# Two attention layers on one core: head scores as fp32 row-tile products instead of stacked fp16 products

## The chip, the cores and the metric

The kernel runs on one core of a Trainium2 chip. The metric is the device time of one execution in microseconds (us); times here are medians of several runs. Engines are named PE (TensorE), ACT (ScalarE), DVE (VectorE), POOL (GpSimd) and SP (the engine that issues most transfers).

## The reference, cut to what matters

The input is x, fp32 of shape (2, 256, 64, 64): two images, 256 channels, N = 4096 positions. Layer 0 is multi-head attention over the positions, layer 1 a non-local block with a pooled key side; the change concerns layer 0 only.

```python
# layer 0: 8 heads of d = 32 channels, n = 4096 positions
qkv = einsum('oc,bchw->bohw', w_qkv, x); q, k, v = split(qkv, 3)
scores = einsum('bhdi,bhdj->bhij', q, k) / sqrt(d)
out = einsum('bhij,bhdj->bhdi', softmax(scores, axis=-1), v)
x = einsum('oc,bchw->bohw', w_proj, out) + x
# layer 1: softmax(theta(x[:, :64])^T maxpool(phi(x[:, 64:]))) times maxpool(g(x)), 1x1 convolution, batch norm, + x
```

## The kernel before, in words

A loop over the two images runs `layer0` and then `layer1`. `layer0` handles the eight heads in two groups of four (g = 0, 1), so there are four rounds of projections and attention in all.

Projections of a group (lines 257 to 388). PE makes q and k in 16 products of 128 channels by 512 positions (line 276) and then v (line 290). ACT writes each q or k piece as fp16 `hi` (line 306) and its square (line 311), and DVE writes the fp16 rest `lo` (line 328). A bound on the largest score is formed from the squares (lines 265, 323, 338 to 346) and stored in `safe`. SP then issues 24 transfers (line 384), which stack hi, lo, hi of every head in rows 0 to 95 of `Qst` and hi, hi, lo in `Kst`: one product over 128 rows then gives hi·hi + lo·hi + hi·lo. POOL clears the rows above (lines 360 to 365). The block ends when the transfers have landed.

Then every engine loads `safe` (line 393). Where the bound is too large, a block finds each query's maximum and puts it in row 96; in the profiled execution it isn't entered, since the page has no row of its lines. It works on the same stacked tensors, so that the attention is the same afterwards.

Attention of a group (lines 469 to 615). Queries go in 8 chunks of 512 (`CH`), keys in 32 tiles of 128 (`JT`). I call one key tile of one chunk a step. A step has four score products, one for each head (line 477, keys as weights, a PSUM bank of 128 keys by 512 queries each), exponentials from PSUM into `P` (line 563), four value products (line 487), and the row sums. The score banks form three buffers of two banks (`buf`, `NBUF` = 3), and one exponential empties one buffer. The value product of head h takes V's 32 columns of that head as weights and writes partitions 32h to 32h+31 of `psO`: four column tiles of the array. `P` is a ring of four key tiles.

Row sums: for most key tiles DVE adds `P` to one of two accumulators (line 595, `acc`), and for the key tiles in `SUM_PE` = 9, 20 and 31 PE sums `P` with a matrix of ones (line 500). At the end of a chunk PE also sums the two accumulators; I call these two groups the flushes. Output and sums are copied out by ACT (lines 534 and 539) inside the next chunk.

Each engine runs its own list in order, and semaphores join them: `s_ready` (scores ready), `s_exp` (exponentials done), `s_pv` (values done), `s_add` (DVE's adds), `s_sum` (PE's sums). PE's list is made from the exponentials' numbers: after exponential o it issues the scores of exponential o + 3, two products at a time (line 474 waits for the exponential that frees that buffer), and the value group of a key tile one exponential after its last one. The first exponential of a step also waits until values, adds and sums have freed the ring slot it writes (lines 552 to 560).

Of the kernel before, what the change touches and what calls it, by code (L numbers as in the profile page):

```python
# [5 lines left out]
ALU = mybir.AluOpType  # L6
# [8 lines left out]
N = H * W  # L15
CT = C // 128
HEADS, D = 8, 32
G = 4
# [11 lines left out]
MW = 1024.0  # L30
# [6 lines left out]
SCORE = 1.0 / (QS * QS * float(D) ** 0.5)  # L37

RING = 4
SIZES = ([2, 2] * 15 + [2, 1, 1]) * 2  # L40
NBUF = 3
NOPS = len(SIZES)
UNITS = JT * G
STARTS = [sum(SIZES[:o]) for o in range(NOPS)]
SUM_PE = [9, 20, 31]
# [18 lines left out]

DONE_BY = [next(o for o in range(NOPS) if STARTS[o] + SIZES[o] >= G * (j + 1)) for j in range(JT)]


VALUES_AT = [d + 1 for d in DONE_BY]
SUMS_AT = [DONE_BY[j] + 2 for j in SUM_PE]
ACC_AT = [NOPS + 1, NOPS + 3]  # L70
O_AT, L_AT = 3, 8
WORK = [(at, "values", j) for j, at in enumerate(VALUES_AT)]
WORK += [(at, "sums", j) for j, at in zip(SUM_PE, SUMS_AT)]
WORK += [(at, "acc", k) for k, at in enumerate(ACC_AT)]
TAIL = max(at for at, _, _ in WORK) + 1 - NOPS
ORDER = sorted((w for w in WORK if w[1] != "values"), key=lambda w: w[0])
FIRST_SUM, LAST_SUM = ORDER[0][1:], ORDER[-1][1:]
assert all(at >= DONE_BY[j] for at, what, j in WORK if what != "acc") and FIRST_SUM[0] == "sums"
assert NOPS % NBUF == 0 and sum(SIZES) == UNITS and SUM_V[:4] == [0, 1, 2, 3]


def conv_seq(nc, x, wqkv, wproj, gw, tw, pw, ww, vectors, biases, out, r_dram, r1_dram):
# [3 lines left out]
    with ExitStack() as root:  # L86
# [35 lines left out]
        safe = sb(root, "safe", [1, 1], I32)  # L122
# [107 lines left out]
        def layer0(b):  # L230
            with ExitStack() as ctx:
                Qst = sb(ctx, "Qst", [128, G, N], F16)
                Kst = sb(ctx, "Kst", [128, G, N], F16)
                V = sb(ctx, "V", [128, JT, G * D])
                s_x = [sem(ctx, f"s_x{c}") for c in range(NC)]
                s_pad = sem(ctx, "s_pad")
                s_mm = sem(ctx, "s_mm")
                s_ev = sem(ctx, "s_ev")
                s_hi = sem(ctx, "s_hi")
                for g in range(NG):  # L240

                    with ExitStack() as c2:
                        hi = [sb(c2, f"hi{k}", [128, N], F16) for k in range(2)]
                        lo = [sb(c2, f"lo{k}", [128, N], F16) for k in range(2)]
# [10 lines left out]
                        s_z = sem(c2, "s_z")  # L255
                        NU = 2 * NC
                        with nc.Block() as block:
# [62 lines left out]
                            def _(dve):  # L320
# [73 lines left out]
                    with ExitStack() as c2, nc.If(known_safe < 1):  # L394
# [9 lines left out]
                        with nc.Block() as block:  # L404
                            @block.gpsimd
                            def _(pool):
                                pool.sem_inc(s_m, 2)
# [669 lines left out]
```

## Time and profile before

| | |
|---|---|
| median of 3 runs | 2954.68 us (2951.5 to 2955.72) |
| span of the profiled execution | 2952.2 us |
| PE, DVE, ACT busy | 2823.0, 2357.6, 2351.8 us |
| instructions | 46817 |

The profiled execution has no time of its own in the list of runs: its span, from the first to the last instruction, is 2952.2 us and lies inside the range of the three runs. The median of the runs is 2.5 us above that span.

The page cuts the span in 40 slices. Engine rows give the busy share in tenths, and PEclk the clock that TensorE was granted:

```profile
PE   7999999999999999788979999999899999997889
DVE  3888888868888888677548888888588888886765
ACT  4999999958999999428449999999599999994284
PEclk9999999999999999899989999999999999999999
DMA  6000000030000000101150000000400000001011
```

Four stretches of attention fill most of the slices, in pairs; the DMA row shows the load of x and the stacking transfers ahead of each. What ends last in the attention is read from the rows further down. A matmul on fp32 data stands as two records in the trace (8192 records of line 487 for 4096 products).

### The profile page before, as it was taken

The page shows a single profiled execution, that of the slowest core. Times are in us where ns is not written, and L with a number is a line of the kernel's source. Part 1 is how long each engine was busy: PE and PEld are TensorE (multiplying, and loading weights), DVE is VectorE, ACT ScalarE, POOL GpSimd, SP SyncE. Part 2 cuts the span into 40 slices and gives each one's busy share as a digit, 9 for nine tenths or more (in the row PEclk, how much of TensorE's full clock was granted, in tenths as well). Part 3 has the DMA queues.
Part 4 walks back from the last instruction along what each step waited for, and adds up shares of the span by engine and source line. Part 5 has one row for each costly group of instructions (what it writes and reads, how often), then busy time and mean ns, then how long its engine had stood idle before and what let it go on. Part 6 is the DMA issues. An engine that isn't in the chain of part 4 may idle for free. (4 is left out here: it accounts for less than half of the span.)

```text
span 2952.2 us, 46817 instructions
## 1 busy us (share of the span) xinstructions
PE 2823.0 (96%) x16210; PEld 812.3 (28%) x16218; DVE 2357.6 (80%) x1478; ACT 2351.8 (80%) x2618; POOL 115.1 (4%) x148
## 2 busy tenths in 40 slices
PE   7999999999999999788979999999899999997889
PEld 4222222242222222233442222222422222222334
DVE  3888888868888888677548888888588888886765
ACT  4999999958999999428449999999599999994284
POOL 3000000010000000001030000000100000000010
PEclk9999999999999999899989999999999999999999
DMA  6000000030000000101150000000400000001011
GB/s 162 1 0 0 0 0 0 1 82 6 1 0 0 0 0 0 46 25 44 39 147 1 0 0 0 0 0 1 86 1 1 0 0 0 0 1 57 14 44 43
DMA packets 29171, 59.40 MB, mean 20 GB/s; under 512 B 11872, under 2 KB 12960, under 8 KB 25632
## 3 DMA queue, kind: packets, MB, share of 16 engines
q1 hardware_dynamic: 29088, 58.33, 7.3%
q8 instruction: 48, 0.79, 0.1%
q14 instruction: 35, 0.29, 0.0%
HBM read 22.88 MB, written 8.68 MB: 11 GB/s over the span
## 5 line engine op out<-in xcount | busy, mean ns | idle before, releaser
L563 ACT ACTIVATE P<-scores 128x1024 f32<-128x1024 f32 (+1 forms) x2112 | 1990.7, 1001 | 172.0 <-PE scores L477 155.6
L595 DVE TENSOR_TENSOR acc<-acc,P 128x2048 f32<-128x2048 f32 x800 | 1776.9, 2283 | 53.4 <-ACT P L563 50.6
L477 PE MATMUL scores<-Qst,Kst 128*128 (+1 forms) x4096 | 1090.8, 385 | 21.9 <-PEq L128 16.1
L487 PE MATMUL psOL<-P,V 128*32 128x512 f32 x8192 | 1090.4, 605 | 0.0
L477 PEld LDWEIGHTS scores<-Qst,Kst 128*128 128x128 f16 x4096 | 313.3, 98 | 1194.2 <-ACT P L563 752.4
L595 DVE TENSOR_TENSOR acc<-P 128x2048 f32<-128x2048 f32 x64 | 146.8, 2293 | 226.1 <-ACT P L563 119.3
L487 PEld LDWEIGHTS psOL<-P,V 128*32 128x32 f32 x8192 | 162.1, 108 | 432.2 <-ACT P L563 327.7
L276 PE MATMUL scores<-X,wq_sb 128*128 128x512 f32 x256 | 124.0, 614 | 29.2 <-DMA X<-in_x 25.4
L997 DVE SCALAR_TENSOR_TENSOR Pl<-O,Ph 128x1536 f16<-128x1536 f32 (+1 forms) x48 | 75.9, 1581 | 65.7 <-ACT Ph L970 65.7
L963 ACT ACTIVATE O<-scores 128x1536 f32<-128x1536 f32 (+1 forms) x48 | 62.4, 1300 | 71.1 <-PE scores L898 71.1
L708 PE MATMUL scores<-O,wp_sb 128*128 128x512 f32 x128 | 64.7, 655 | 43.6 <-DVE O L665 43.6
L328 DVE SCALAR_TENSOR_TENSOR lo<-scores,hi 128x512 f16<-128x512 f32 x64 | 44.2, 691 | 77.1 <-ACT hi L306 77.1
L500 PE MATMUL psOL<-P,ones 128*32 128x512 f32 x768 | 102.2, 604 | 0.0
L910 PE MATMUL psOL<-Pl,GTh 128*128 128x512 f16 x256 | 97.1, 379 | 0.0
L910 PE MATMUL psOL<-Ph,GTh 128*128 128x512 f16 x256 | 97.1, 379 | 0.0
L910 PE MATMUL psOL<-Ph,GTl 128*128 128x512 f16 x256 | 97.1, 379 | 0.0
L697 ACT ACTIVATE Yh<-X 128x512 f16<-128x512 f32 x32 | 20.1, 630 | 89.6 <-DVE X L685 89.6
L306 ACT ACTIVATE hi<-scores 128x512 f16<-128x512 f32 x64 | 38.2, 597 | 53.2 <-PE scores L276 53.2
L276 PEld LDWEIGHTS scores<-X,wq_sb 128*128 128x128 f32 x256 | 50.1, 197 | 86.9 <-issue 58.8
L360 POOL MEMSET Qst<- 1x16384 f16 x2 | 27.5, 13746 | 1156.8 <-POOLq L128 1156.8
L970 ACT ACTIVATE Ph<-O 128x1536 f16<-128x1536 f32 (+1 forms) x48 | 64.3, 1341 | 2.8
L500 PE MATMUL psOL<-acc,ones 128*32 128x512 f32 x512 | 66.6, 598 | 0.0
(107 smaller groups left out, 1342.1 us busy)
## 6 DMA issues: line engine op xcount, KB each, us to landing
X<-in_x SPq DMA_DIRECT2D x16, 512.0 KB, 7.8
Qst<-hi SPq DMA_DIRECT2D x32, 256.0 KB, 5.0
Kst<-hi SPq DMA_DIRECT2D x32, 256.0 KB, 5.1
R<-att_inv SPq DMA_DIRECT2D x32, 256.0 KB
out<-res SPq DMA_DIRECT2D x32, 256.0 KB, 2.0
Qst<-lo SPq DMA_DIRECT2D x16, 256.0 KB, 5.4
Kst<-lo SPq DMA_DIRECT2D x16, 256.0 KB, 4.7
R<-pool_inv SPq DMA_DIRECT2D x2, 2048.0 KB, 6.8
```

Of the source, the lines that this page charges most:

```text
L276: last = nc.tensor.matmul(slot(u), w, X[:, t, c * CH:(c + 1) * CH], start=(t == 0), stop=(t == CT - 1))
L328: nc.vector.scalar_tensor_tensor(out=lo[k][:, c * CH:(c + 1) * CH], in0=slot(u), scalar=QS, in1=hi[k][:, c * CH:(c + 1) * CH], op0=ALU.mul ...
L477: last = nc.tensor.matmul(buf[o % NBUF][:, k * CH:(k + 1) * CH], Kst[:, h, j * 128:(j + 1) * 128], Qst[:, h, bass.ds(c * CH, CH)], start=T ...
L487: last = nc.tensor.matmul(psO[h * D:(h + 1) * D, :], V[:, j, h * D:(h + 1) * D], P[:, (j % RING) * G + h, :], start=(j == 0), stop=(j == J ...
L500: last = nc.tensor.matmul(psL[h * D:(h + 1) * D, :], ones[:], src, start=(what, j) == FIRST_SUM, stop=(what, j) == LAST_SUM)
L563: nc.scalar.activation(P[:, r:r + SIZES[o], :], s3, ACT.Exp, scale=SCORE).then_inc(s_exp, 1)
L595: nc.vector.tensor_tensor(acc[:, sum_of(n)], old, new, ALU.add).then_inc(s_add, 1)
L708: last = nc.tensor.matmul(slot(u), wp_sb[:, k, t * 128:(t + 1) * 128], O[:, k, c * CH:(c + 1) * CH], start=(k == 0), stop=(k == CT - 1))
L910: last = nc.tensor.matmul(psOL[:, t * CH:(t + 1) * CH], w[:, m, ts], v[:, p, m, :], start=(n == 0), stop=(n == 3 * MT - 1))
L963: nc.scalar.activation(P32[:, p, ms, :], bank[o % 2][:, 0:SZ[k] * CH].rearrange("p (u n) -> p u n", n=CH), ACT.Exp, scale=SCORE1).then_inc ...
L970: nc.scalar.activation(Ph[:, p, ms, :], P32[:, p, ms, :], ACT.Copy, scale=PS).then_inc(s_h, 1)
L997: nc.vector.scalar_tensor_tensor(out=Pl[:, p, ms, :], in0=P32[:, p, ms, :], scalar=PS, in1=Ph[:, p, ms, :], op0=ALU.mult, op1=ALU.subtract ...
```

## The change

- q and k are kept as fp32 in `Q` and `K` (128 rows: four heads of 32). ACT no longer writes `hi`; it squares the PSUM piece directly, and DVE then copies the piece. The 24 stacking transfers of a group and POOL's clearing are gone.
- The score product of head h reads rows 32h to 32h+31 of `K` and `Q` in fp32: the four heads lie on the four row tiles of the array. Each writes all 128 partitions of its own PSUM bank.
- PE's list goes by whole steps: wait for the first exponential of the step before, issue all four score products of the step, signal `s_ready` once, and then the value group of the step two before (`LAG` = 2). Sums and flushes stand directly behind a value group. `SUM_PE` has four key tiles (7, 15, 23, 31) for three, and DVE has 26 adds in a chunk for 27.
- Every exponential covers two heads: 64 in a chunk for 66. ACT's and PE's loops over chunks are written out.
- The attention always runs in its fast form. The guard comes behind it: where the bound is too large, a separate attention with maxima recomputes the group, head by head.

```diff
-SCORE = 1.0 / (QS * QS * float(D) ** 0.5)
+SCORE = 1.0 / float(D) ** 0.5
...
-SIZES = ([2, 2] * 15 + [2, 1, 1]) * 2
-SUM_PE = [9, 20, 31]
+LAG = 2
+SUM_PE = [7, 15, 23, 31]
...
+NSUM = len(SUM_PE) + 2
+ACC_AFTER = [JT + 1, JT + 2]
+O_AT, L_AT = 3, 9
...
-    Qst = sb(ctx, "Qst", [128, G, N], F16)
-    Kst = sb(ctx, "Kst", [128, G, N], F16)
+    Q = sb(ctx, "Q", [128, N])
+    K = sb(ctx, "K", [128, N])
     V = sb(ctx, "V", [128, JT, G * D])
...
                     for u in range(NU):
                         k, c = divmod(u, NC)
+                        cs = slice(c * CH, (c + 1) * CH)
                         act.wait_ge(s_mm, u + 1)
-                        nc.scalar.activation(hi[k][:, c * CH:(c + 1) * CH], slot(u), ACT.Copy,
-                                             scale=QS).then_inc(s_hi, 1)
                         if u >= 2:
                             act.wait_ge(s_nm, u - 1)
-                        act.wait_ge(s_hi, u + 1)
-                        nc.scalar.activation(sq[u % 2][:], hi[k][:, c * CH:(c + 1) * CH], ACT.Square
-                                             ).then_inc(s_sq, 1)
+                        nc.scalar.activation(sq[u % 2][:], slot(u), ACT.Square).then_inc(s_sq, 1)
...
-                        dve.wait_ge(s_hi, u + 1)
-                        nc.vector.scalar_tensor_tensor(
-                            out=lo[k][:, c * CH:(c + 1) * CH], in0=slot(u), scalar=QS,
-                            in1=hi[k][:, c * CH:(c + 1) * CH],
-                            op0=ALU.mult, op1=ALU.subtract).then_inc(s_ev, 1)
+                        cs = slice(c * CH, (c + 1) * CH)
+                        dve.wait_ge(s_sq, u + 1)
+                        nc.vector.tensor_copy(QK[k][:, cs], slot(u)).then_inc(s_ev, 1)
...
                         sp.dma_start(Ls[:, g - 1, NC - 1, :], L[0:128:D, :]).then_inc(s_st, 16)
-                        n += 16
-                    for k, dst, parts in ((0, Qst, (hi[0], lo[0], hi[0])), (1, Kst, (hi[1], hi[1], lo[1]))):
-                        sp.wait_ge(s_ev, NC * (k + 1))
-                        for h in range(G):
-                            for r, part in enumerate(parts):
-                                sp.dma_start(dst[r * D:(r + 1) * D, h, :],
-                                             part[h * D:(h + 1) * D, :]).then_inc(s_st, 16)
-                                n += 16
-                    sp.wait_ge(s_st, n)
-            end_phase(c2, s_x + [s_pad, s_mm, s_ev, s_hi, s_st, s_sq, s_nm, s_nx, s_vm, s_ve, s_b, s_z])
...
-                    def scores(before, o, c):
-                        if before is not None:
-                            pe.wait_ge(s_exp, before)
-                        for k in range(SIZES[o]):
-                            j, h = divmod(STARTS[o] + k, G)
-                            last = nc.tensor.matmul(buf[o % NBUF][:, k * CH:(k + 1) * CH],
-                                                    Kst[:, h, j * 128:(j + 1) * 128],
-                                                    Qst[:, h, bass.ds(c * CH, CH)], start=True, stop=True)
+                    def scores(c, j):
+                        cs = slice(c * CH, (c + 1) * CH)
+                        for h in range(G):
+                            rows = slice(h * D, (h + 1) * D)
+                            dst = buf[(2 * (c * JT + j) + h // 2) % NBUF]
+                            last = nc.tensor.matmul(dst[:, (h % 2) * CH:(h % 2 + 1) * CH],
+                                                    K[rows, j * 128:(j + 1) * 128], Q[rows, cs],
+                                                    start=True, stop=True)
                         last.then_inc(s_ready, 1)
+                    def values(c, j, waits):
+                        if waits:
+                            pe.wait_ge(s_exp, c * 2 * JT + 2 * j + 2)
...
+                    def flush(c, k):
+                        pe.wait_ge(s_add, (c + 2) * ADDS - 1 + k)
+                        for h in range(G):
+                        last.then_inc(s_sum, 1)
+                    for n in range(LAG):
+                        if n:
+                            pe.wait_ge(s_exp, 2 * n - 1)
+                        scores(0, n)
+                    for n in range(NC * JT + max(ACC_AFTER) - JT + 1):
+                        c, i = divmod(n, JT)
+                        if n + LAG < NC * JT:
+                            pe.wait_ge(s_exp, 2 * (n + LAG) - 1)
+                            scores(*divmod(n + LAG, JT))
+                        if n < NC * JT:
+                            values(c, i, n + LAG >= NC * JT)
+                            if i in SUM_PE:
+                                direct_sums(c, i)
+                        if n >= JT and i + JT in ACC_AFTER:
+                            flush(c - 1, ACC_AFTER.index(i + JT))
                 @block.scalar
                 def _(act):
...
+                    def chunk(c):
+                        for o in range(2 * JT):
+                            if o == O_AT and c:
...
-                            act.wait_ge(s_ready, c * NOPS + o + 1)
-                            u0 = STARTS[o]
-                            j0, j1 = u0 // G, (u0 + SIZES[o] - 1) // G
-                            if j0 != j1 or u0 % G == 0:
...
+                            j, pair = divmod(o, 2)
+                            act.wait_ge(s_ready, c * JT + j + 1)
+                            if pair == 0:
+                                act.wait_ge(s_pv, c * JT + j + 1)
...
+                                if j >= RING:
+                                    act.wait_ge(s_add, (c + 1) * ADDS + adds_through(j - RING))
...
+                            r = (j % RING) * G + 2 * pair
+                            s3 = buf[(2 * JT * c + o) % NBUF].rearrange("p (u n) -> p u n", n=CH)
+                            nc.scalar.activation(P[:, r:r + 2, :], s3, ACT.Exp, scale=SCORE).then_inc(s_exp, 1)
+                    for c in range(NC):
+                        chunk(c)
...
+        known_safe = nc.values_load(safe[0:1, g:g + 1], min_val=0, max_val=1)
+        with ExitStack() as c2, nc.If(known_safe < 1):
```

PE's list in the middle of a chunk of before: `scores` is the PSUM tensor of the scores, `Qst` and `Kst` the stacked tensors, `psOL` holds outputs and sums.

```order
L477 MATMUL scores<-Qst,Kst 128x512 [waits s_exp]
L477 MATMUL scores<-Qst,Kst 128x512
L474 REGISTER_ALU
L477 MATMUL scores<-Qst,Kst 128x512 [waits s_exp]
L477 MATMUL scores<-Qst,Kst 128x512
L487 MATMUL psOL<-P,V 32x512 [waits s_exp]
L487 MATMUL psOL<-P,V 32x512 x3
L474 REGISTER_ALU
```

And where a chunk ends in the changed kernel (line 366 scores, 377 values, 387 direct sums, 395 flushes):

```order
L366 MATMUL scores<-Q,K 128x512 [waits s_exp]
L366 MATMUL scores<-Q,K 128x512 x3
L377 MATMUL psOL<-P,V 32x512 x4
L387 MATMUL psOL<-P,ones 32x512 x4
L366 MATMUL scores<-Q,K 128x512 [waits s_exp]
L366 MATMUL scores<-Q,K 128x512 x3
L377 MATMUL psOL<-P,V 32x512 [waits s_o_free]
L377 MATMUL psOL<-P,V 32x512 x3
L366 MATMUL scores<-Q,K 128x512 [waits s_exp]
L366 MATMUL scores<-Q,K 128x512 x3
L377 MATMUL psOL<-P,V 32x512 x4
L395 MATMUL psOL<-acc,ones 32x512 [waits s_add]
```

Two pairs of scores, each with its own wait for an exponential and its own signal, have become one group of four behind one wait; the value group no longer waits for an exponential, since the wait ahead of the scores covers it. A sum group lengthens the step in which it stands, between two score groups.

ACT's list in the projections, before:

```order
L306 ACTIVATE hi<-scores 128x512 [waits s_mm]
L311 ACTIVATE sq<-hi 128x512 [waits s_hi,s_nm]
L306 ACTIVATE hi<-scores 128x512 [waits s_mm]
L311 ACTIVATE sq<-hi 128x512 [waits s_hi,s_nm]
L316 COPY V<-scores 128x512 [waits s_ve,s_vm] x4
```

and in the changed kernel:

```order
L289 ACT_TABLE_LOAD
L289 ACTIVATE sq<-scores 128x512 [waits s_mm] x2
L289 ACTIVATE sq<-scores 128x512 [waits s_nm,s_mm] x14
L293 COPY V<-scores 128x512 [waits s_ve,s_vm] x4
L237 UNCONDITIONAL_BRANCH
```

One activation of the two for each piece is gone.

## Rows read from the trace of the kernel before

**Rows 1.** The page, busy us (share of span), instructions of each engine

```profile
PE 2823.0 (96%) x16210; PEld 812.3 (28%) x16218; DVE 2357.6 (80%) x1478; ACT 2351.8 (80%) x2618; POOL 115.1 (4%) x148
```

**Rows 2.** The page, costliest groups: busy us, mean ns of one, idle before

```profile
L563 ACT ACTIVATE P<-scores 128x1024 f32<-128x1024 f32 (+1 forms) x2112 | 1990.7, 1001 | 172.0 <-PE scores L477 155.6
L595 DVE TENSOR_TENSOR acc<-acc,P 128x2048 f32<-128x2048 f32 x800 | 1776.9, 2283 | 53.4 <-ACT P L563 50.6
L477 PE MATMUL scores<-Qst,Kst 128*128 (+1 forms) x4096 | 1090.8, 385 | 21.9 <-PEq L128 16.1
L487 PE MATMUL psOL<-P,V 128*32 128x512 f32 x8192 | 1090.4, 605 | 0.0
```

**Rows 3.** Busy by window: length, PE, PEld, DVE, ACT, POOL, PEclk, DMA share, GB/s

```profile
145.00:206.00 61.00, 61.00 (x379) 14.34 (x376) 57.89 (x27) 57.51 (x63) 0.00 (x0) 1.00 0.00 0
```

**Rows 4.** Timeline, one attention step: start us, length us, engine, line, operation

```profile
301.44 1.06 PE L487 MATMUL psOL<-P,V 128*32 128x512 f32 x8
...
302.44 1.04 PE L477 MATMUL scores<-Qst,Kst 128*128 x4
...
303.41 0.64 PE L487 MATMUL psOL<-P,V 128*32 128x512 f32 x4
```

**Rows 5.** Timeline at the end of a chunk of queries

```profile
207.06 1.07 PE L500 MATMUL psOL<-P,ones 128*32 128x512 f32 x8
...
207.94 1.04 PE L500 MATMUL psOL<-acc,ones 128*32 128x512 f32 x8
...
208.92 0.60 PE L477 MATMUL scores<-Qst,Kst 128*128 x2
209.05 2.29 DVE L595 TENSOR_TENSOR acc<-P 128x2048 f32<-128x2048 f32 x1 [3.77 <-PE psOL L500]
```

**Rows 6.** Line 534, first attention: register step before each output copy

```profile
L534 ACTq FUSED_REGOPS  x7: 60/60/66, 138.5 to 547.5; - x7
```

**Rows 7.** Timeline, four first halves of a value group alone

```profile
301.44 0.64 PE L487 MATMUL psOL<-P,V 128*32 128x512 f32 x4
```

**Rows 8.** Lines 563, 487, 595: duration ns min/median/max, first and last start us

```profile
L563 ACT ACTIVATE P<-scores x2112: 588/1023/1152, 70.8 to 2680.8; 128x1024 f32<-128x1024 f32 x192
...
L487 PE MATMUL psOL<-P,V x8192: 592/593/677, 74.2 to 2682.0; 128*32 128x512 f32 x200
...
L595 DVE TENSOR_TENSOR acc<-P x64: 2291/2293/2295, 74.6 to 2623.6; 128x2048 f32<-128x2048 f32 x64
```

**Rows 9.** Line 276, fp32 with 128 weight columns, first instruction after idling

```profile
L276 PEld LDWEIGHTS scores<-X,wq_sb x1: 187/187/187, 617.8 to 617.8; 128*128 128x128 f32 x1
L276 PE MATMUL scores<-X,wq_sb x1: 668/668/668, 617.9 to 617.9; 128*128 128x512 f32 x1
```

**Rows 10.** Timeline, ScalarE waiting for a product of the projections

```profile
34.73 1.02 PE L276 MATMUL scores<-X,wq_sb 128*128 128x512 f32 x2
...
35.78 0.60 ACT L306 ACTIVATE hi<-scores 128x512 f16<-128x512 f32 x1 [0.61 <-PE scores L276]
```

**Rows 11.** Timeline, TensorE waiting for an exponential at the start of the attention

```profile
70.78 1.94 ACT L563 ACTIVATE P<-scores 128x1024 f32<-128x1024 f32 x2 [5.84 <-PE scores L477]
...
72.77 0.10 PEld L477 LDWEIGHTS scores<-Qst,Kst 128*128 128x128 f16 x1 [0.37 <-ACT P L563]
```

**Rows 12.** Busy time by window, in the projections

```profile
30.00:40.00 10.00, 9.95 (x26) 4.49 (x26) 6.44 (x10) 6.47 (x11) 9.49 (x1) 1.00 0.39 79
```

**Rows 13.** Line 384, first projections: from DMA issue to landing

```profile
DMA to landing us min/median/max: 3.1/5.0/6.0
```

**Rows 14.** Timeline between the projections and the first attention

```profile
62.90 1.30 SPq L384 DMA_DIRECT2D Kst<-lo  x1
...
64.36 0.58 ACT L316 COPY V<-scores 128x512 f32<-128x512 f32 x1 [2.48 <-PE scores L290]
...
69.71 0.61 PE L477 MATMUL scores<-Qst,Kst 128*128 128x512 f16 x1 [5.39 <-issue]
```

**Rows 15.** Busy time by window, first 3 us of the attention

```profile
69.70:72.70 3.00, 2.99 (x8) 1.00 (x8) 0.00 (x0) 1.92 (x3) 0.00 (x0) 0.50 0.02 5
```

More of the change, by code:

```diff
@@ L29 @@
 QS = 16.0
-MW = 1024.0
 MW1 = 256.0
@@ L61, in sum_of @@
     return n % 2 if n < 2 else (n + ADDS) % 2
[L65 to L79, printed above, removed]
+NSUM = len(SUM_PE) + 2
+ACC_AFTER = [JT + 1, JT + 2]
+O_AT, L_AT = 3, 9
+assert SUM_V[:4] == [0, 1, 2, 3] and JT % RING == 0
 def conv_seq(nc, x, wqkv, wproj, gw, tw, pw, ww, vectors, biases, out, r_dram, r1_dram):
@@ L121, in conv_seq @@
         heads = sb(root, "heads", [128, 128], BF16)
-        safe = sb(root, "safe", [1, 1], I32)
+        safe = sb(root, "safe", [1, NG], I32)
         L = sb(root, "L", [128, CH])
@@ L503, in row_sums @@
                                     last.then_inc(s_sum, 1)
-                                def work(c, at):
-                                    for when, what, j in WORK:
-                                        if when == at:
-                                            values(c, j) if what == "values" else row_sums(c, what, j)
-                                def inside(c, last):
-                                    for o in range(TAIL, NOPS + TAIL):
-                                        if o + NBUF < NOPS:
-                                            scores(c * NOPS + o + 1, o + NBUF, c)
-                                        elif not last:
-                                            scores(c * NOPS + o + 1, o + NBUF - NOPS, c + 1)
-                                        work(c, o)
-                                        if o >= NOPS and not last:
-                                            work(c + 1, o - NOPS)
@@ L521, in _ @@
-                                for o in range(NBUF):
-                                    scores(None, o, 0)
-                                for o in range(TAIL):
-                                    scores(o + 1, o + NBUF, 0)
-                                    work(0, o)
-                                with pe.Fori(0, NC - 1) as c:
-                                    inside(c, False)
-                                inside(NC - 1, True)
+                                def flush(c, k):
+                                    pe.wait_ge(s_add, (c + 2) * ADDS - 1 + k)
+                                    for h in range(G):
+                                        last = nc.tensor.matmul(psL[h * D:(h + 1) * D, :], ones[:], acc[:, k, h, :],
+                                                                start=False, stop=(k == 1))
+                                    last.then_inc(s_sum, 1)
@@ L539, in sums_out @@
                                     nc.scalar.copy(L[:], psL).then_inc(s_l_free, 1)
-                                def chunk(c, first):
-                                    for o in range(NOPS):
-                                        if o == O_AT and not first:
+                                def chunk(c):
+                                    for o in range(2 * JT):
+                                        if o == O_AT and c:
                                             output_out(c - 1)
-                                        if o == L_AT and not first:
+                                        if o == L_AT and c:
@@ L563, in chunk @@
-                                        nc.scalar.activation(P[:, r:r + SIZES[o], :], s3, ACT.Exp,
-                                                             scale=SCORE).then_inc(s_exp, 1)
-                                chunk(0, True)
-                                with act.Fori(1, NC) as c:
-                                    chunk(c, False)
+                                                act.wait_ge(s_sum, (c + (j >= RING)) * NSUM + SUM_PE.index(before) + 1)
+                                            if j >= RING:
+                                                act.wait_ge(s_add, (c + 1) * ADDS + adds_through(j - RING))
+                                            else:
+                                                act.wait_ge(s_add, c * ADDS + adds_through(j - RING + JT))
```

226 lines of the change are left out of this document (125 added, 101 removed).

## The prediction

> **What bounds the kernel now.** I read the page's busy row first: PE is busy for 96% of the span, DVE and ACT for 80% [rows 1]. That alone doesn't name the bound, so I took the costliest groups: exponentials, adds, scores and values of the attention make up nearly all of it, and ACT's idle time ahead of the exponentials is put down to PE's scores [rows 2]. Then a window inside the attention: in 61.00 us PE is busy for all 61.00, DVE for 57.89, ACT for 57.51, at a granted clock of 1.00 [rows 3]. The attention is bound by PE, with ACT and DVE some 5% behind.
>
> The timeline of one step shows what PE spends: a value group starts at 301.44, the four scores at 302.44, the next value group at 303.41 [rows 4]. So 1.00 us for values and 0.97 for scores, 1.97 together. A sum group directly behind another group on column tiles takes 207.94 - 207.06 = 0.88 [rows 5], so about 0.12 of the value group's 1.00 is the passage to the scores. Seven register steps ahead of the output copies lie between 138.5 and 547.5 [rows 6]: a chunk takes 409.0 / 6 = 68.2 us. There are 8 x 4 = 32 chunks, 2182 us of the 2952.2.
>
> In this kernel the scores of a buffer are asked for as soon as one exponential has freed it, and two other buffers are full or being filled meanwhile. That slack is why PE never waits.
>
> **The score group.** Four fp32 products on row tiles are not in the trace. The nearest rows are the value groups: four fp32 products on column tiles. Their four first halves start together, as one entry of 0.64 us [rows 7], and the whole group of eight records is over 1.06 us after its start [rows 4]. I take row tiles to run side by side in the same way. One difference: a value product loads 32 weight columns, a score product 128. After an idle stretch, the first fp32 record with 128 columns lasts 668 ns, where the first of a value group lasts at most 618 [rows 8, 9]; the weight load of 187 ns shows through by 0.05 us more. So from first start to last end a score group takes 1.06 + 0.05 = 1.11 us, and of PE's time 1.00 + 0.05 = 1.05. Bounds: from below a group can't be over before two halves have followed each other, 1.02 (two fp32 records in a row on the full array) [rows 10]. From above, all eight records one behind the other, at 0.43 each (1.02 - 0.59), 3.6 us. I take 1.11, since the column group is the same work on the same array, and keep both ends.
>
> For scores, then, PE gains nothing: four fp16 products cost 0.97, the fp32 group 1.05. By PE's work alone a step is 2.05 for 1.97.
>
> **The new loop, which I put above PE's work.** The scores of a step wait for the first exponential of the step before, since they need two of the three buffers at once. That exponential can't be followed by the next step's first one until the whole group is done. So there is a ring: exponential 1.02 (the median) [rows 8], from its end to PE's next load 0.05 (70.78 + 1.94 = 72.72, load at 72.77) [rows 11], score group 1.11, from its end to ACT's start 0.03 (34.73 + 1.02 = 35.75, start at 35.78) [rows 10]. Sum 2.21 us for a step. PE's 2.05 fits into it, ACT's second exponential too (it runs under the score group). The wait for the second exponential that the value group had is gone at no gain.
>
> **Steps with sums.** Six steps of a chunk carry a sum or a flush behind the values, one more than before. PE has 1.05 + 1.00 + 0.88 = 2.93 there, above 2.21, and the next score group is late by the rest; the ring has no slack to win it back. A chunk is 26 x 2.21 + 6 x 2.93 = 57.5 + 17.6 = 75.1.
>
> **The start of a chunk.** DVE's first add waits for the first flush. Counted from the start of that step's scores the flush begins at 1.05 + 0.88 = 1.93 and ends at 2.99; the add then takes 2.29 [rows 8] and ends at 5.32. The first exponential of the next step overwrites what it reads, so it starts at 5.35, not at 2.93 + 1.11 + 0.03 = 4.07. It ends at 6.37, the next scores start at 6.42, where PE alone would have been ready at 2 x 2.93 = 5.86. That is 0.6 us a chunk. Behind it DVE has 26 adds in 32 steps; 26 adds of 2.29 are 59.5 us, below the chunk's, so no other add is waited for. The output and sum copies on ACT are covered: one stands beside a sum step, the other beside this stall.
>
> A chunk comes to 75.1 + 0.6 = 75.7, against 68.2: 7.5 more, times 32 is +240 us. Two exponentials fewer in a chunk count for nothing, since ACT isn't what ends last, and the written-out loops add only instructions to fetch, while the DMA engines are at 0.00 here [rows 3].
>
> **Projections.** PE is busy for 9.95 of 10 us there [rows 12], so ACT's missing activation and DVE's plain copy in place of the subtraction are hidden by PE. DVE's copy waits for ACT's square; a piece then needs two instructions one behind the other where it had hi and then lo, so nothing gets later. If that cover were gone it would be some 0.6 us a piece, 40 us in all, at the outside. POOL's clearing is waited for by nobody. What shows is the end: the last product's copy starts at 64.36 and takes 0.58, to 64.94; the last stacking transfer is issued at 62.90 and lands 3.1 to 6.0 us later, by the median of 5.0 at 67.9; the attention's scores start at 69.71 [rows 13, 14]. Without transfers the block ends at 64.94 instead of 67.9: 3.0 us a round, four rounds, -12. The load of `safe` and its branch move behind the attention and cost there what they cost here. After the idle 5.4 us the first 3 us of the attention run at a granted 0.50, the 1.2 GHz level [rows 15]; if the shorter gap keeps 2.4 GHz, 1.5 us a round come back at most. I take 3 us for the four.
>
> **Sum.** 2952.2 + 240 - 12 - 3 = 3177 for the span; with the 2.5 us between span and median of the runs, 3180.
>
> **A rule against the change.** The trace has the first halves of a column group starting together [rows 7], so the two halves of one product don't stand behind each other ahead of the next head. The Trainium skill, "TensorE: Matmul & The Clock Gate", Part 3 (The mechanism), says that matmuls start and end strictly in program order. Taken with a product whose two halves are neighbours in that order, it would make the fp32 heads nearly serial; this trace speaks against it for column tiles, and no run here shows it for row tiles. What it would do is the first rival below, priced from rows.
>
> **Rivals.**
>
> Row tiles serial. Each head's second half needs its own weights; if the array can't hold four heads' halves on row tiles, the records follow each other. Latency 7 x 0.43 + 0.59 + 0.08 = 3.68, ring 1.02 + 0.05 + 3.68 + 0.03 = 4.78; steps with sums 3.44 + 0.17 + 1.00 + 0.88 = 5.49; chunk 26 x 4.78 + 6 x 5.49 = 157, +89 x 32 = +2850, time about 5790. For it: nothing like this group is in the trace. Against it: rows 7. 8%.
>
> Two at a time. Latency 3 x 0.43 + 0.67 = 1.96, ring 3.06, steps with sums 1.72 + 0.17 + 1.88 = 3.77; chunk 79.6 + 22.6 = 102, +34 x 32 = +1090, time about 4030. 6%; whatever lies between this and my range has another 7%.
>
> Not slower. The mechanism is that the row group is shorter than its column twin and the ring isn't felt: PE's work alone then sets the step. With a score group at 0.95 (no visible weight load, a cheap passage) a chunk is 32 x 1.95 + 6 x 0.88 = 67.7, -0.5 x 32 = -16, with the -15 above a time of about 2924. It decides only where the ring stays below (68.2 - 17.0) / 26 = 1.97 us, that is a group latency below 0.87. Two halves in a row take 1.02 on the full array [rows 10], so I give it 3%.
>
> The change isn't what it says. If the guard were now taken, the separate attention would run head by head behind each group, with a product, an exponential and a value product one behind the other 256 times a head: far above my range. The bound is the same quantity in another scale, and before it wasn't taken. 1%, inside the cases above my range.
>
> **How the numbers follow.** My case has 75%. Its own spread: latency 1.06 (no extra weight load) gives a ring of 2.16, 56.2 + 17.3 + 0.6 = 74.1 a chunk, +189 - 15, so 3129; latency 1.02 gives 72.7 a chunk and 3084. Every tenth of a us more in the group is 3.2 us a chunk, +102 in all: 1.25 us is 3323. Range 3105 to 3330. What lies above (serial, pairs, in between, guard) has 22% and is mostly far away; I leave it out. A measurement of this kernel tells 0.2% from no change, some 6 us: slower by more than that 96%, within 1%, faster 3%.
>
> **What would show it.** Right: a first exponential of each step every 2.2 us, DVE and ACT each idle a little in every step, PE's idle time ahead of the scores ended by an exponential, about 0.15 us each; steps of 2.9 us at key tiles 7, 15, 23, 31 and at the two flushes, one of them with a stall of half a us more; chunks of 75 to 76 us. The eight records of a score group start in two bursts of four. Wrong: a PE without idle time in the attention (then the group is the bound), records of a score group that start one after another, a chunk near 68, or rows of the separate attention.

## The result and the profile after

| | before | after |
|---|---|---|
| median of the runs (4 each) | 2953.09 us | 3267.18 us (3263.93 to 3270.33) |
| ratio, 95% interval | | 1.1066, 1.1053 to 1.108 |
| span of the profiled execution | 2952.2 us | 3268.4 us |
| PE, DVE, ACT busy | 2823.0, 2357.6, 2351.8 us | 2985.4, 2331.0, 2305.7 us |

The change costs 314 us, 10.7%. The forecast was 3180 (3105 to 3330): the direction, the cause and the range were right, the time 87 us low. The page of the changed kernel, its busy row and costliest groups (columns as in [rows 1, 2]; line 447 exponentials, 477 adds, 366 scores, 377 values):

```profile
PE 2985.4 (91%) x20562; PEld 840.3 (26%) x20570; DVE 2331.0 (71%) x1446; ACT 2305.7 (71%) x2490; POOL 32.8 (1%) x140
...
L447 ACT ACTIVATE P<-scores 128x1024 f32<-128x1024 f32 x2048 | 1988.9, 1023 | 479.1 <-PE scores L366 414.0
L477 DVE TENSOR_TENSOR acc<-acc,P 128x2048 f32<-128x2048 f32 x768 | 1750.3, 2291 | 263.9 <-ACT P L447 261.9
L366 PE MATMUL scores<-Q,K 32*128 32x512 f32 x8192 | 1173.2, 642 | 158.1 <-ACT P L447 55.2
L377 PE MATMUL psOL<-P,V 128*32 128x512 f32 x8192 | 1092.7, 606 | 0.8 <-ACT P L447 0.8
L366 PEld LDWEIGHTS scores<-Q,K 32*128 32x128 f32 x8192 | 321.1, 183 | 1077.9 <-ACT P L447 1070.8
L477 DVE TENSOR_TENSOR acc<-P 128x2048 f32<-128x2048 f32 x64 | 146.7, 2292 | 334.9 <-PE psOL L395 286.0
```

The exponentials cost what they did (1988.9 us for 1990.7), but ACT's idle time ahead of them has gone from 172.0 to 479.1. Now PE is idle as well ahead of the scores (158.1, before 21.9), and the weight loads of the scores wait for an exponential for 1070.8 us in all, before for 752.4: two engines that wait for each other. The window of [rows 3] in the changed kernel shows it as three engines none of which is full, at full clock:

```profile
145.00:206.00 61.00, 57.50 (x444) 13.04 (x440) 46.67 (x22) 48.70 (x53) 0.00 (x0) 1.00 0.01 1
```

The timeline of one step, which answers to [rows 4] (start us, length us, engine, line; in brackets the idle time before and what ended it):

```profile
311.18 1.96 ACT L447 ACTIVATE P<-scores 128x1024 f32<-128x1024 f32 x2
...
312.28 1.14 PE L366 MATMUL scores<-Q,K 32*128 32x512 f32 x8 [0.19 <-ACT P L447]
...
313.35 1.06 PE L377 MATMUL psOL<-P,V 128*32 128x512 f32 x8
313.49 1.94 ACT L447 ACTIVATE P<-scores 128x1024 f32<-128x1024 f32 x2 [0.35 <-PE scores L366]
...
314.57 1.14 PE L366 MATMUL scores<-Q,K 32*128 32x512 f32 x8
...
315.77 1.94 ACT L447 ACTIVATE P<-scores 128x1024 f32<-128x1024 f32 x2 [0.35 <-PE scores L366]
```

Read it as a ring. Scores start at 312.28 and end at 313.42; the first exponential starts at 313.49, ends 1.02 later at 314.51, and the next scores start at 314.57: 2.29 us, where before a step was 1.97. Values (313.35 to 314.41) lie beside it and are over before the scores may start.

The start of a chunk, with both flushes (line 395) and the first add that waits for one [rows 5]:

```profile
303.41 1.14 PE L366 MATMUL scores<-Q,K 32*128 32x512 f32 x8
...
305.37 1.04 PE L395 MATMUL psOL<-acc,ones 128*32 128x512 f32 x8
...
306.34 1.14 PE L366 MATMUL scores<-Q,K 32*128 32x512 f32 x8
306.48 2.29 DVE L477 TENSOR_TENSOR acc<-P 128x2048 f32<-128x2048 f32 x1 [9.57 <-PE psOL L395]
...
308.88 1.02 ACT L447 ACTIVATE P<-scores 128x1024 f32<-128x1024 f32 x1 [2.32 <-DVE acc L477]
...
309.96 1.14 PE L366 MATMUL scores<-Q,K 32*128 32x512 f32 x8 [0.62 <-ACT P L447]
...
386.60 1.02 ACT L447 ACTIVATE P<-scores 128x1024 f32<-128x1024 f32 x1 [2.33 <-DVE acc L477]
```

A step with a flush takes 306.34 - 303.41 = 2.93, the next one 3.62, since the exponential at 308.88 waits for the add that ends at 308.77. The same exponential stands at 386.60 in the next chunk: 77.72 us a chunk, for 68.2 before.

The edges of the attention: into it (against [rows 14, 15]) and out of it, into the projections of the second group.

```profile
63.87 0.59 ACT L293 COPY V<-scores 128x512 f32<-128x512 f32 x1 [2.48 <-PE scores L270]
...
65.44 1.14 PE L366 MATMUL scores<-Q,K 32*128 32x512 f32 x8 [1.61 <-PEq L112]
...
687.15 1.90 PE L395 MATMUL psOL<-acc,ones 128*32 128x512 f32 x16
...
695.79 2.93 PE L256 MATMUL scores<-X,wq_sb 128*128 128x512 f32 x3 [6.75 <-issue]
```

```profile
65.40:68.40 3.00, 1.82 (x16) 0.66 (x16) 0.00 (x0) 1.76 (x2) 0.00 (x0) 1.00 0.03 8
...
695.80:705.20 9.40, 9.35 (x18) 4.15 (x20) 2.44 (x4) 1.79 (x3) 0.00 (x0) 0.79 0.01 3
```

The first attention starts 4.3 us earlier (65.44 for 69.71), at full clock where before it began at 0.50. In the other three the clock still falls, some 2.5 us after the first score product; the second one shows it:

```profile
748.00:752.25 4.25, 3.13 (x17) 0.52 (x9) 1.12 (x1) 2.08 (x3) 0.00 (x0) 0.50 0.00 0
```

And between an attention and the next projections TensorE is now idle for 6.75 us, and the projections behind it run at a mean granted clock of 0.79: their first 16 records take 9.34 us. In the trace of before, the same place looks like this, with 7.32 us for the 16 records:

```profile
617.86 7.32 PE L276 MATMUL scores<-X,wq_sb 128*128 128x512 f32 x16 [1.69 <-PEq L128]
```

### The profile page after: what moved, and what is told of

It is laid out like the page before. It is cut to its first block and busy times, and to the rows that moved or that the text cites. A ratio compares the mean times of both kernels' runs of the same rounds, so it can differ in the third digit from the quotient of the medians.

```text
span 3268.4 us, 50045 instructions
## 1 busy us (share of the span) xinstructions
PE 2985.4 (91%) x20562; PEld 840.3 (26%) x20570; DVE 2331.0 (71%) x1446; ACT 2305.7 (71%) x2490; POOL 32.8 (1%) x140
## 5 line engine op out<-in xcount | busy, mean ns | idle before, releaser
L447 ACT ACTIVATE P<-scores 128x1024 f32<-128x1024 f32 x2048 | 1988.9, 1023 | 479.1 <-PE scores L366 414.0
L477 DVE TENSOR_TENSOR acc<-acc,P 128x2048 f32<-128x2048 f32 x768 | 1750.3, 2291 | 263.9 <-ACT P L447 261.9
L366 PE MATMUL scores<-Q,K 32*128 32x512 f32 x8192 | 1173.2, 642 | 158.1 <-ACT P L447 55.2
L366 PEld LDWEIGHTS scores<-Q,K 32*128 32x128 f32 x8192 | 321.1, 183 | 1077.9 <-ACT P L447 1070.8
L387 PE MATMUL psOL<-P,ones 128*32 128x512 f32 x1024 | 133.3, 592 | 0.0
L289 ACT ACTIVATE sq<-scores 128x512 bf16<-128x512 f32 x64 | 38.2, 597 | 114.3 <-PE psOL L245 66.9
L306 DVE COPY Q<-scores 128x512 f32<-128x512 f32 x32 | 22.1, 692 | 79.3 <-ACT sq L289 79.3
L673 DVE TENSOR_TENSOR O<-O,R 128x1024 f32<-128x1024 f32 x16 | 19.6, 1226 | 62.7 <-DMA R<-att_inv 62.7
```

The source lines that it names most:

```text
L366: last = nc.tensor.matmul(dst[:, (h % 2) * CH:(h % 2 + 1) * CH], K[rows, j * 128:(j + 1) * 128], Q[rows, cs], start=True, stop=True)
L387: last = nc.tensor.matmul(psL[h * D:(h + 1) * D, :], ones[:], P[:, (j % RING) * G + h, :], start=(j == SUM_PE[0]), stop=False)
L447: nc.scalar.activation(P[:, r:r + 2, :], s3, ACT.Exp, scale=SCORE).then_inc(s_exp, 1)
L477: nc.vector.tensor_tensor(acc[:, sum_of(n)], old, new, ALU.add).then_inc(s_add, 1)
```

## The experiments

The theory: a ring of one exponential and one whole score group sets the step; every step with sums adds 0.64 us to it. The rival readings: the fp32 row-tile products as such are what costs (PE's work), or the additions on DVE hold, or the code around the attention. "Changed kernel" is the kernel after the change. The edits are abridged here, in part to a line of words. Each run is compared with the kernel before on the same chip.

**Guard cut to a stub.**

```diff
-                        for h in range(G):          # separate attention, head by head
+                        for h in range(1):
-                                    for it in range(JT):   /   for j in range(JT):
+                                    for it in range(1):    /   for j in range(2):
```

> The changed kernel with the guarded block cut to a stub (the separate attention is left out but for one head and a few products, and isn't entered); the load of the bound and the branch stay. Theory: TensorE's 4.26 us on that branch and the projections' slow first 9 us come from the jump over some 1000 written-out instructions. Then the branch falls to under 0.5 us, four times 3.9 us, and the two projections behind a first attention win another 2 us each: about -20 us on 3267, so 3247. Rival: the idle time there is the small transfer of the sums or the barrier, then nothing changes (3267). The attention itself stays at chunks of 77.7 us.

3254.53 us, ratio 1.1028 (1.1009 to 1.1046), so 12.7 less than the changed kernel (10.6 between the two profiled executions): less gain than the 20 us expected, but at the place named. In its timeline and in a window of 7 us behind it:

```profile
694.05 3.27 PE L256 MATMUL scores<-X,wq_sb 128*128 128x512 f32 x7 [2.72 <-issue]
```

```profile
694.00:701.00 7.00, 6.95 (x17) 3.15 (x18) 1.97 (x3) 1.79 (x3) 0.00 (x0) 1.00 0.02 5
```

Idle 2.72 for 6.75, and the granted clock stays at 1.00. The chunk is the same 77.71: the guard has no part in the 305 us.

The expectation counted four passages, and PE's record of the branch does fall at all four (3.4 to 4.7 us in the changed kernel, under 0.4 here). But only the two that lead into projections pay for it, with 4.0 and 4.5 us of idle time and 2.0 us each behind it at the lower clock. At the two that lead into layer 1, TensorE's next product waits for DVE's output (14.15 and 14.21 us idle, here 13.59 and 15.85), and the branch is covered.

**The new loop, with the old fp16 products.**

```diff
 # kernel before (stacked fp16, its guard and projections), with the changed kernel's lists
-SIZES = ([2, 2] * 15 + [2, 1, 1]) * 2 ; SUM_PE = [9, 20, 31]
+LAG = 2 ; SUM_PE = [7, 15, 23, 31] ; ACC_AFTER = [JT + 1, JT + 2]
+    for h in range(G): matmul(dst, Kst[:, h, keys], Qst[:, h, cs])   # four behind one wait
```

> The kernel before, its stacked fp16 tensors and guard kept, but with the changed kernel's lists in the attention: four scores behind one wait and one signal, value group two steps later, sums at key tiles 7, 15, 23, 31, loops written out. Theory (the ring sets the step): exponential 1.02 + 0.05 + group latency 3 x 0.214 + 0.39 = 1.03 + 0.07 = 2.18 us a step, 2.85 in the six with sums, 0.7 stall: 74.5 us a chunk, +200 on 2953, about 3155. Rival (what costs is the fp32 work on row tiles and the sixth sum group): without row tiles only the sum group is left, 32 x 0.88 = +28, about 2981.

3147.21 us, ratio 1.0665 (1.0647 to 1.0682). So some 196 us come from the new lists (order, sums of four key tiles) alone, with not one fp32 score product in them; the fp32 products and all the rest account for 120. A step is 2.15, one with sums 2.82 in its trace, so that the fourth sum group has 0.67 x 32 = 21 of the 196. The long step at the start of a chunk is there too, with the same 3.62:

```profile
301.80 1.04 PE L462 MATMUL scores<-Qst,Kst 128*128 128x512 f16 x4
...
304.34 1.02 ACT L543 ACTIVATE P<-scores 128x1024 f32<-128x1024 f32 x1 [2.35 <-DVE acc L573]
...
305.42 1.04 PE L462 MATMUL scores<-Qst,Kst 128*128 128x512 f16 x4 [0.73 <-ACT P L543]
```

**All four heads on one row tile.** This measures the serial rival.

```diff
-        rows = slice(h * D, (h + 1) * D)
+        rows = slice(0, D)                    # scores only
```

> As e1_small_guard, but all four score products read rows 0 to 31, so that they share one row tile (the scores of heads 1 to 3 are those of head 0). If the four row tiles really work side by side, this takes that away: eight records 0.43 apart, group latency about 3.7, ring 4.85, chunk about 157 us, time near 5780. If the row tiles were no help, the time stays near 3250.

9896.68 us (one run), far above what was expected. The page's clock row and a window inside the attention say why:

```profile
PEclk6555555556555555555965555555565555555559
```

```profile
1000.00:1060.00 60.00, 60.00 (x120) 17.66 (x119) 13.75 (x6) 13.57 (x14) 0.00 (x0) 0.53 0.00 0
...
1008.40:1011.00 2.60, 2.60 (x8) 1.10 (x6) 0.00 (x0) 0.00 (x0) 0.00 (x0) 1.00 0.00 0
```

PE is busy for 60.00 of 60 us and its granted clock is near the 1.2 GHz level. Eight records follow each other there 0.853 apart, 7.12 of PE's time for the group (7.19 to the end of the last), and 0.43 apart in the short stretches at 2.4 GHz (1008.40 to 1011.00), which is the pitch that the rival was priced with. So the pitch of serial products was priced rightly and their clock was missed. The converse is what counts: eight records in 1.14 us do come from four row tiles working side by side.

**Three fp16 row-tile terms for one fp32 product** (with the stub guard).

```diff
-    matmul(dst, K[rows, keys], Q[rows, cs])
+    for kk, qq in ((hi_k, hi_q), (hi_k, lo_q), (lo_k, hi_q)):
+        for h in range(G): matmul(dst[h], kk[rows, keys], qq[rows, cs])   # accumulated in PSUM
```

> As e1_small_guard, but q and k are kept as fp16 hi and lo (as before, without stacked copies), and each head's score is hi x hi + hi x lo + lo x hi on its row tile, term by term over the four heads. Ring theory: group latency 2 x 0.214 + 0.41 = 0.84, ring 1.02 + 0.05 + 0.84 + 0.07 = 1.98, steps with sums 0.76 + 1.00 + 0.88 = 2.64, stall 0.7, chunk 68.0, time 3247 - 9.7 x 32 = 2937. Rival (only TensorE's work counts): 32 x 1.76 + 6 x 0.88 = 61.6 a chunk, time about 2740.

2935.74 us, ratio 0.9949 (0.9932 to 0.9965): as expected to 1.3 us, which is in part luck, since the sum started from 3247 for the stub guard kernel and that took 3254.53. Against it 319 us are gone, 312 of them in 32 chunks, by a score group that is over after 0.83 us for 1.14:

```profile
319.97 0.39 PE L371 MATMUL scores<-hi 32*128 32x512 f16 x4
...
320.20 0.38 PE L371 MATMUL scores<-lo,hi 32*128 32x512 f16 x4
...
320.42 0.38 PE L371 MATMUL scores<-hi,lo 32*128 32x512 f16 x4
...
320.73 1.06 PE L382 MATMUL psOL<-P,V 128*32 128x512 f32 x8
```

The step is 1.96 (2.29) and the chunk 67.95 (77.71), shorter by 9.76: a plain step by 0.33, which is about the latency that went (0.31), a step with sums by 0.31, which is PE's time for the group (0.76 for 1.07), and the step of 3.62 by nothing.

**The same terms, head by head.**

```diff
-    for term in terms: for h in range(G): matmul(...)
+    for h in range(G): for term in terms: matmul(...)
```

> As t2_three_terms, with the same 12 products head by head in place of term by term. If TensorE starts products strictly in the order of the program, the third term of one head and the first of the next are the only ones side by side: last start 3 x 0.435 + 0.43 = 1.73, latency 2.11, ring 3.26, chunk about 108 us, time near 4230. If it may pass over a product whose tile is busy, as one might read from the two bursts of four in the fp32 groups, the time stays at 2936.

2990.71 us (one run): near the kernel without strict order, 1240 below the strict one.

```profile
300.66 0.42 PE L371 MATMUL scores<-hi 32*128 32x512 f16 x4 [0.17 <-ACT P L452]
...
300.88 0.41 PE L371 MATMUL scores<-lo,hi 32*128 32x512 f16 x4
...
301.10 0.41 PE L371 MATMUL scores<-hi,lo 32*128 32x512 f16 x4
```

The first terms of the four heads start within 0.03 us of each other (300.658 to 300.692), and the second terms, which the program puts ahead of the next head's first, start from 300.884. Records on different row tiles are not held to the program's order. That bears on the rule that the forecast weighed, the one of the Trainium skill, "TensorE: Matmul & The Clock Gate", Part 3 (The mechanism), on start and end in strict program order: this run doesn't agree with it for row tiles. Neither do the bursts of the changed kernel, if the two halves of a product are neighbours in that order. The order isn't free, though: the chunk is 69.42 for 67.95.

**Flushes one step earlier** (on the stub guard kernel).

```diff
-ACC_AFTER = [JT + 1, JT + 2]
+ACC_AFTER = [JT, JT + 1]
```

> As e1_small_guard, with both flushes one step earlier (behind the value groups of key tiles 0 and 1 of the next chunk). If the 3.62 us step at the start of a chunk is the first add waiting for the first flush, and the exponential for the add, then the stall of 0.69 us goes: about -0.65 x 32 = -21 us on 3254, so 3233. If that long step is something else (the two copies on ScalarE), nothing changes, or it gets longer.

3236.61 us, ratio 1.0965 (1.0947 to 1.0983), 17.9 less than the stub guard kernel, whose interval it doesn't touch. The flush now stands a step ahead, and the exponential behind it waits for PE alone:

```profile
303.91 1.14 PE L366 MATMUL scores<-Q,K 32*128 32x512 f32 x8
...
305.12 1.94 ACT L447 ACTIVATE P<-scores 128x1024 f32<-128x1024 f32 x2 [0.99 <-PE scores L366]
...
306.83 1.14 PE L366 MATMUL scores<-Q,K 32*128 32x512 f32 x8
...
309.12 1.14 PE L366 MATMUL scores<-Q,K 32*128 32x512 f32 x8 [0.15 <-ACT P L447]
```

The chunk is 77.04 for 77.71: the stall was worth 0.67 a chunk, 21 us in all.

**One fp16 term only** (on the stub guard kernel).

```diff
-    Q, K fp32
+    Q, K fp16, one product a head
```

> As e1_small_guard, with q and k rounded to fp16 and one product a head (less exact scores). Ring: group latency 0.03 + 0.38 = 0.41, so 1.02 + 0.05 + 0.41 + 0.07 = 1.55, now below ScalarE's two exponentials (about 1.8) and VectorE's 26 adds (58.2). So the ring lets go and the chunk is 60 to 62 us: 3254 - 16 x 32 = about 2740. If something else than the group's latency held the step at 2.29, it stays above that.

2767.22 us (one run), 27 above the expectation. The group is over after 0.39 us, and a step is 1.83, not shorter:

```profile
306.15 0.39 PE L366 MATMUL scores<-Q,K 32*128 32x512 f16 x4 [0.44 <-ACT P L447]
```

A group shorter by 0.75 took only 0.45 off the step. By the ring it would be 1.54. The exponentials end 0.917 us apart in the trace, one behind the other, and twice that is the step: here ACT is the bound. Only behind a step with sums, where ACT has caught up, does the trace have a step of 1.53, which is the ring's. The timeline's 1.02 for one is longer than the pitch, since neighbours overlap by a tenth of it.

**Three steps with sums.**

```diff
-SUM_PE = [7, 15, 23, 31]
+SUM_PE = [9, 20, 31]
```

> The changed kernel with three steps instead of four whose sums go to TensorE (after steps 9, 20 and 31 in place of 7, 15, 23 and 31); VectorE takes one addition more in a chunk, 29 probabilities in place of 28. Everything else as in the changed kernel. By the ring a step with sums is 0.64 us longer than one without (2.925 against 2.286 in its trace), so 32 chunks lose 32 x 0.64 = 20.5 us: 3245 to 3249 us. If VectorE's addition (about 2.1 us in a step of 2.29 us) is what holds, the extra one is on the path (it has to catch up where a step with sums gave it air) and the time stays at 3262 to 3270 us or rises.

3246.56 us, ratio 1.1004 (1.0986 to 1.1023): 20.6 less than the changed kernel, as the ring has it. Chunk 77.08, shorter by 0.63. DVE's extra addition costs nothing.

**Guard for one head of four.**

```diff
-                        for h in range(G):
+                        for h in range(1):
```

> The changed kernel with the separate attention behind the guard built for one head of the four (its loops otherwise whole; the inputs never take the guard, so no work that is executed is left out). The stub took 12.7 us off the changed kernel, of which the trace showed about 4.0 us at each passage from an attention to projections (idle of TensorE before the first projection 6.75 us, with the stub 2.72 us). If the price follows the length of the code that is passed over, a quarter of the code costs a quarter of it: some 3 us more than the stub, 3257 to 3259 us, idle 3.7 us. If it is a step, paid as soon as the target lies out of what is at hand, one head costs what four cost: 3266 to 3268 us, idle 6.7 us. If code that is passed over within a few hundred instructions is free: 3254 to 3256 us, idle 2.7 us.

3261.62 us, ratio 1.1056 (1.1038 to 1.1074). The times alone can't place it, since its interval touches both neighbours'. The idle time can:

```profile
695.98 3.78 PE L256 MATMUL scores<-X,wq_sb 128*128 128x512 f32 x4 [6.00 <-issue]
```

6.00 us, with a quarter of the code, where the whole guard has 6.75 and the stub 2.72. A price by length would be 3.7. With the stub PE's two records of that branch last 0.36 and 0.38 us. In the changed kernel and with one head they are (min/median/max in ns), and last the jump back of the loop over images in the kernel before, which spans the whole loop body (its minimum is the end of the loop, where no jump follows):

```profile
L238 PEldq COMPARE_BRANCH  x2: 4261/4486/4711, 691.5 to 2322.5; - x2
```

```profile
L238 PEldq COMPARE_BRANCH  x2: 3652/3759/3866, 692.3 to 2316.5; - x2
```

```profile
L1045 PEldq COMPARE_BRANCH  x2: 79/1870/3662, 1481.4 to 2952.1; - x2
```

So it is a step: paid when the passage is long, with little or nothing more for four times the length (the whole guard has 3.66 and 4.43 us in the kernel with three sums, 3.48 and 3.62 in the combined version below). The kernel before paid it once already, 3.66 us at 1481.4. Where between the stub and one head it sets in wasn't tried.

**The combined version,** first with the stub guard and then with a whole one.

```diff
 # three terms, and
-SUM_PE = [7, 15, 23, 31] ; ACC_AFTER = [JT + 1, JT + 2]
+SUM_PE = [15, 31]        ; ACC_AFTER = [JT, JT + 1]
```

> As t2_three_terms (ring 1.96, steps with sums 2.61), with sums at key tiles 15 and 31 only and both flushes one step earlier: two steps of 2.61 fewer, no stall. Chunk 28 x 1.96 + 4 x 2.61 = 65.3 to 66.4, against 67.5: 1.2 to 2.2 us a chunk, 2936 becomes 2866 to 2898. Rival: VectorE, with 28 adds of 2.24 = 62.6 and a later start, becomes the bound; then the time is at or above 2936.

2877.65 us, ratio 0.9756 (0.9739 to 0.9772). The window of [rows 3] in it:

```profile
145.00:206.00 61.00, 57.41 (x632) 12.43 (x632) 58.73 (x28) 58.93 (x62) 0.00 (x0) 1.00 0.01 2
```

The three engines are nearly even, at 57 to 59 of 61. A plain step is still 1.96, as in the three-term kernel, so the ring still sets it; two steps with sums less and no stall bring the chunk from 67.95 to 65.65.

> The combined version (fp16 high and low parts, three row-tile products a head, two steps with sums, early flush) with its separate attention behind the guard built whole: that attention puts the high and the low part of q and k together again in fp32 for the head it works on. The stub version took 2877.65 us. If the price of code that is passed over is what the changed kernel paid over its stub (12.7 us for the four guards), 2887 to 2893 us, which still beats the kernel before by 2%; if the longer code costs nothing here, 2876 to 2879 us.

2885.30 us, ratio 0.9783 (0.9766 to 0.9799). That is 2 us below the expected range: by the medians the whole guard costs 7.7 us here, against 12.7 in the changed kernel, but its runs lie between 2879.20 and 2889.46 and its interval touches that of the version with the stub, so the size of the difference is uncertain. And this version beats the kernel before by 2.2%.

## Why the forecast was right, and where 87 us were missing

**What bounds it.** Right. With the stub guard, exchanging only the score products took 0.31 off the group's latency and 0.33 off the step (2.286 to 1.958); exchanging only the lists in the kernel before turned 68.2 into 73.91 a chunk.

**Score group.** Four row tiles side by side, two bursts of four: starts at 301.128 to 301.148 and 301.662 to 301.682. Forecast 1.11 to the end and 1.05 of PE's time, measured 1.140 and 1.071.

**Ring.** Forecast 2.21, measured 2.286. Of the 0.076, 0.03 is the group and 0.037 the way from its end to the exponential, which took 0.067 and not the 0.03 read in the projections [rows 10]: the row was of another wait. Twenty-six steps a chunk make 2.0 us of this, 63 us in all. This is the mis-sized term that made most of the miss: of the 91 us between the forecast span (3177) and the measured one, 63 are this, some 3 the stall, 9 the first chunks and 17 what lies outside the attention (both below). The terms of a few hundredths look small against an exponential of 1.02; a ring takes each of them 832 times.

**Steps with sums.** Forecast 2.93, measured 2.925, and a step less of them gave 0.63 a chunk where 2.925 - 2.286 = 0.64 was due.

**Stall at the start of a chunk.** Forecast 0.6, measured 0.69 in the trace, 0.67 by removing it. The way from the add's end to the exponential was 0.11 and not 0.03.

So a chunk of 77.71 consists of 25 steps of 2.286, one of 2.32, five of 2.925 and one of 3.62; 32 chunks are +305 where +240 was forecast. From its first score product to its last flush an attention takes 623.6 to 626.0 us, the four together 2501.6 for 2187.3: +314. The other 9 us lie in the first chunks. Before, the first chunk of each attention was 2.7 to 3.4 us shorter than the others; now it is shorter by 2.7 in the first attention and by 0.2 to 0.3 in the other three. Those three are the ones in which the clock falls to 0.50 soon after the start, with score groups of 1.82 and 2.09 us for 1.14; it costs 2.4 us each time. Which attentions it strikes changes from kernel to kernel: all four with the stub guard, one with the guard for one head.

**Projections.** The step that failed is the sentence that the load of `safe` and its branch "cost there what they cost here". All outside the attention was to be 15 us shorter, and it is 1.9 longer (766.8 for 764.9). With the stub it is 753.8, that is 11 shorter. The saved transfers are real: TensorE's idle time ahead of the four attentions fell from 21.5 to 6.5 us, 15.0 where 12 was forecast. The 3 us from a better clock didn't come: half-clock stretches at the start of an attention were four before, and are three in the changed kernel and four with the stub. The rest lies behind the attention, where TensorE's idle time, over the four, rose from 28.7 to 42.2 us. Of these 13.5 us, 6.0 are there with the stub too (34.7), and 7.5 are the passage over the separate attention. PE's branch has a record of 4.26 us there, where the branch of before had 0.38. Behind the longer gap the projections start at a granted clock of 0.79, which costs 2.0 us at each of the two places. The forecast took the price of a short branch for a long one, though the trace of before had a long one with 3.66 us, the jump back of the loop over images. What in such a branch takes the time isn't settled: that one head's code costs nearly what four do speaks against the length as such, and the runs show no more than that.

**Rivals.** Serial row tiles: their pitch was right, but the four tiles don't behave so. Two at a time: excluded by the bursts. Not slower: its point was a latency below 0.87; with 0.83 the three-term kernel has a chunk of 67.95 for 68.2, so the point where the ring decides was placed well. No row of the separate attention is in the trace.

## What to carry to other kernels

When several products are put behind one wait, ask whether the engine that frees their buffer can go on while they run; if it can't, the two make a ring and every latency in it is paid in each step, wherever the busy shares stand. Take the latencies of a ring from waits of the same pair of engines and the same kind of instruction, since hundredths of a microsecond count hundreds of times. And code that is only passed over isn't free: look at the idle time of each engine behind a long block that isn't entered, and at the clock of what follows.

## What the runs showed of the hardware

- Row tiles run fp32 products side by side as column tiles do: eight records of four heads within 1.14 us, 0.43 apart only where all use one tile.
- Records on different row tiles start out of the program's order: first terms of four heads within 0.03 us (300.658 to 300.692), ahead of second terms (from 300.884) that stand before them.
- With one row tile of four at work, TensorE was at a granted 0.53 (near the 1.2 GHz level) in a window in which it was busy for 60.00 of 60 us; with all four it was at 1.00 in one in which it was busy for 57.50 of 61.00.
- Passing over a long block that isn't entered left TensorE idle for 5.6 to 7.0 us ahead of the projections, with a short block 2.4 to 2.9; PE's branch had records of 3.4 to 4.7 us and under 0.4. The jump back over the whole loop body took 3.66 in the kernel before.
